# A four-layer graph network on one core: the packed edge table is built and stored before the node rows, from ScalarE's queue

## The chip, the cores and the metric

The kernel is one program on one core of one Trainium2 chip. The metric is the device time of the whole program in microseconds (us); lower is better. TensorE is called PE below, VectorE DVE, ScalarE ACT, GpSimd POOL and SyncE SP. SP, ACT and POOL each can start DMA transfers; the 16 DMA engines of the core carry them.

## The reference, cut to what matters

There are 3125 nodes with 128 features and 53125 directed edges, sorted by destination. Four layers run one after the other; the first one is the one around which the change lies:

```python
h = jnp.maximum(_layernorm(x, axis=-1), 0.0)
msg_in = jnp.concatenate([h[src], h[dst], edge_attr], axis=-1)
msgs = jnp.maximum(msg_in @ mW1 + mb1, 0.0) @ mW2 + mb2
agg = jax.ops.segment_sum(msgs, dst, num_segments=num_nodes)
agg = agg / jnp.clip(cnt, 1.0)[:, None]
...
# layers 2 to 4: segment sums of h[src] over the same edges, unweighted or weighted by edge_weight
```

The later layers use a dense count matrix and a dense weight matrix (nodes by nodes) that the kernel builds from the edge list while it runs the first layer.

## The kernel before

The edges are cut into 104 **quads** of 512 edges (NQ = 104, QE = 512); a quad has four gathers of 128 rows each. The program has two stages around the change.

**Start.** SP loads `x` (25 tiles of 128 nodes, in seven groups j = 0 to 6, the last one of 53 rows) and parts of the edge arrays. ACT's queue loads the two halves of `mW1` and the first 96 rows of `src_l` and `dst_l`. A row of these tiles is one quad: 512 edges and a halo of 112 (624 words, 2496 bytes). Row 103 is shorter. So each of the three arrays (`src`, `dst`, edge weight) comes in as a transfer of 96 rows (QA = NQ // 16 * 16), one of 7 rows and one of 1 row. DVE computes variances (`variance`, `norm`), ACT the roots (`root`), POOL the normed rows (`normed_rows`), PE transposes them (`make_T0`), ACT reads them (`read_T0`), PE multiplies by the first half of `mW1` (`make_P`), ACT reads that (`read_P`) and SP stores it to `p_rows` (`store_P`). Then DVE turns the indices into `idx` (`s_edE`), and POOL may gather from `p_rows`.

**The edge table.** For the dense matrices each edge is packed with its weight in `pw` (4096 * dst + src, and the weight). POOL copies the weight in, DVE the packed index (`s_pk` counts both), and one DMA of 3328 rows of 1024 bytes writes overlapping windows of it to `edge_windows`:

```python
sp.wait_ge(s_pk, 2)
sp.wait_ge(s_pt, 16 * NC)
sp.dma_start(win_tab.rearrange("(q j) c -> q j c", j=32), windows_of(pw_i)).then_inc(s_pst, 16)
```

POOL reads seven groups of it back with seven gathers, in its loop over quads behind the gathers of quad 2 (`if q == 2`), when the store has landed (`s_pst`) and the positions are known (`s_sidx`). DVE decodes them (`unpack`), PE transposes the result (`keys`, 21 transposes), and from quad 4 on each quad also makes one block of the matrices (`blocks`).

**Sweep.** In quad q, PE does `pre(q + 1)` (which waits for the four gathers of quad q + 1 and sums them with the destination part), one half of `blocks(q - 4)`, `seg(q)`, `q_window(q + 4)`, and the other half. ACT does `relu`, DVE adds (`add`, which waits for `q_window`), copies and makes one-hot tiles. Two orders matter: PE runs `keys` at the head of q == 2, behind `pre(2)` and `seg(1)`; DVE runs `unpack` at q == 1, behind `add(0)`, the copy of window 4 and `onehot(2)`. Each engine runs its own instructions in the order in which they are written, with waits on semaphores between them.

Of the kernel before, what the change touches and what calls it, by code (L numbers as in the profile page):

```python
# [5 lines left out]
def gnn_kernel(nc, x_in, src_in, dst_in, ea_in, ew_in, mW1, mb1, mW2, mb2, uW1, ub1, uW2, ub2,  # L6
# [4 lines left out]
    ALU = mybir.AluOpType  # L11
# [3 lines left out]
    N, D = x_in.shape  # L15
# [76 lines left out]
    with ctx:  # L92
# [424 lines left out]
        def _(sp):  # L517
            def tail(tile, array, arrived):
                sp.dma_start(tile[QA:NQ - 1, 0:HALO],
                             bass.AP(array.tensor, QA * QE, [[QE, NQ - 1 - QA], [1, HALO]])).then_inc(arrived, 16)  # L520
                sp.dma_start(tile[NQ - 1:NQ, 0:QR],
                             array[(NQ - 1) * QE:E].rearrange("(a e) -> a e", a=1)).then_inc(arrived, 16)

            def body(tile, array, arrived):
                sp.dma_start(tile[0:QA, 0:HALO], bass.AP(array.tensor, 0, [[QE, QA], [1, HALO]])).then_inc(arrived, 16)

# [11 lines left out]
            sp.wait_ge(s_pad, 6)  # L538
# [40 lines left out]
            sp.wait_ge(s_pad, 7)  # L579
# [158 lines left out]
        def _(pool):  # L738
# [28 lines left out]
            normed_rows(0)  # L767
            pool.memset(zerob[:, :], 0.0).then_inc(s_con, 1)
            normed_rows(1)
            count_up(iota_k[:, :, :], [[1, KCOLS], [0, 2]], base=KBASE).then_inc(s_con, 1)  # L770
            normed_rows(2)
            count_up(iota_l[:, :, :], [[1, 128], [0, 2]]).then_inc(s_con, 1)
            count_up(npio[:, :], [[0, 1]], step=-1).then_inc(s_con, 1)
            normed_rows(3)
            for j in range(4, NC):
                normed_rows(j)

            pool.wait_ge(s_w, 48)
            pool.tensor_copy(pw[:, :, 1], w_l).then_inc(s_pk, 1)
# [8 lines left out]
            for q in range(NQ):  # L788
# [4 lines left out]
                if q == 2:  # L793
# [67 lines left out]
        def _(act):  # L861
# [7 lines left out]
            for k in range(2):  # L869
                act.dma_start(w_m1[:, k, :], mW1[k * D:k * D + D, :]).then_inc(s_wt, 16)  # L870
            for tile, array, arrived in ((src_l, src_in, s_src), (dst_l, dst_in, s_dst)):
                act.dma_start(tile[0:QA, 0:HALO], bass.AP(array.tensor, 0, [[QE, QA], [1, HALO]])).then_inc(arrived, 16)
            act.wait_ge(s_pad, 1)
            for q0, q1 in ((1, QA + 1), (QA + 1, NQ)):
                act.dma_start(prev_i[q0:q1, :], bass.AP(dst_in.tensor, q0 * QE - 2, [[QE, q1 - q0], [1, 2]]))\
                    .then_inc(s_prev, 16)

            act.wait_ge(s_con, 3)
            link(act.activation(sd[:, 0:1], eps[:, 0:1], ACT.Sqrt))

# [35 lines left out]
            pipeline((0, root(0, 0)), (2, read_T0(0)), (3, read_P))  # L916
# [222 lines left out]
        def _(dve):  # L1139
# [7 lines left out]
            dve.memset(prev_i[0:1, :], -1).then_inc(s_pad, 1)  # L1147
            dve.memset(x[:, NT - 1, :], 0.0).then_inc(s_pad, 1)
# [3 lines left out]
            dve.memset(ea_l[QA:NQ, :], 0.0).then_inc(s_pad, 1)  # L1152
# [29 lines left out]

            dve.wait_ge(s_con, 2)
# [12 lines left out]
            dve.wait_ge(s_src, 48)  # L1196
# [819 lines left out]
```

## Time and profile before

| what | value |
|---|---|
| time of the program, median of 3 runs | 1050.0 us (1049.88 to 1053.69) |
| the profiled execution's own time | 1055.58 us |
| its span, first to last instruction | 1053.7 us |
| PE busy (matmul) | 877.1 us, 83% |
| DVE, ACT, POOL busy | 645.6, 503.3, 495.6 us |
| mean granted TensorE clock | 0.963 of full speed |

The span is what the rows below are measured in, from the first instruction. The profiled execution's own time is 1.9 us longer than its span, and 5.6 us longer than the median of the three runs; a sum over rows is made against 1055.58 us and then set beside the median.

### The profile page before, as it was taken

The page shows a single profiled execution, that of the slowest core. Times are in us where ns is not written, and L with a number is a line of the kernel's source. Part 1 is how long each engine was busy: PE and PEld are TensorE (multiplying, and loading weights), DVE is VectorE, ACT ScalarE, POOL GpSimd, SP SyncE. Part 2 cuts the span into 40 slices and gives each one's busy share as a digit, 9 for nine tenths or more (in the row PEclk, how much of TensorE's full clock was granted, in tenths as well). Part 3 has the DMA queues.
Part 4 walks back from the last instruction along what each step waited for, and adds up shares of the span by engine and source line. Part 5 has one row for each costly group of instructions (what it writes and reads, how often), then busy time and mean ns, then how long its engine had stood idle before and what let it go on. Part 6 is the DMA issues. An engine that isn't in the chain of part 4 may idle for free.

```text
span 1053.7 us, 21016 instructions
## 1 busy us (share of the span) xinstructions
PE 877.1 (83%) x7797; PEld 792.2 (75%) x7797; DVE 645.6 (61%) x1759; ACT 503.3 (48%) x1012; POOL 495.6 (47%) x496
## 2 busy tenths in 40 slices
PE   4422887888778787888898888899899999999997
PEld 3422777777777776777887888788788988889786
DVE  5524676867776677667777777787775231213664
ACT  3211455655555555565666666676334300111874
POOL 6457665666666677566666666533411000003111
PEclk9566899999999999999999999999999999999999
DMA  5641355555655558555555555545623787786410
GB/s 145 193 135 45 96 147 147 151 151 149 202 160 147 147 139 138 160 152 157 153 152 148 155 159 153 143 144 169 187 62 141 283 306 285 292 304 206 136 54 23
DMA packets 118795, 169.02 MB, mean 160 GB/s; under 512 B 17248, under 2 KB 85382, under 8 KB 118691
## 3 DMA queue, kind: packets, MB, share of 16 engines
q1 hardware_dynamic: 104405, 138.82, 42.7%
q0 software_dynamic: 13648, 28.21, 10.9%
q8 instruction: 64, 1.05, 0.4%
q10 hardware_dynamic: 638, 0.61, 0.3%
q14 instruction: 40, 0.33, 0.1%
HBM read 109.15 MB, written 58.44 MB: 159 GB/s over the span
## 4 chain that ended last, share of the span: by engine, by line
PE 76%; issue 10%; DMA 4%; DVE 3%; another core or an unknown queue 2%; POOL 2%; ACT 2%; SPq 0%; ACTq 0%; DVEq 0%
PE ps L1883 13%; PE ps L1868 12%; PE ps L1740 12%; PE ps L1706 9%; PE ps L1720 9%; PE ps L1707 8%; PE ps L1738 4%; DMA edge_windows<-room 2%; PE ps L1693 2%; PE ps L1852 2%; POOL h L763 1%; PE ps L1755 1%; DMA x<-in_x 1%; DMA room<-dst_row 1%
## 5 line engine op out<-in xcount | busy, mean ns | idle before, releaser
L784 POOL DMA_INDIRECT room<-p_rows,idx x416 | 413.1, 993 | 235.2 <-issue 99.5
L1740 PE MATMUL ps<-room 128*128 128x100 bf16 x2400 | 193.8, 208 | 59.0 <-issue 57.5
L1740 PEld LDWEIGHTS ps<-room 128*128 128x128 bf16 x2400 | 152.0, 98 | 83.4 <-issue 79.2
L947 ACT ACTIVATE room<-ps 128x400 uint8<-128x400 f32 x200 | 101.1, 506 | 219.1 <-remote 209.6
L1706 PE MATMUL ps<-room,ident 128*128 128x128 f32 x832 | 172.0, 289 | 32.4 <-ACT g L922 15.4
L1738 PE MATMUL ps<-room 128*128 128x100 bf16 x800 | 155.6, 209 | 31.8 <-issue 29.2
L1707 PE MATMUL ps<-room 128*128 128x128 f32 x832 | 164.6, 280 | 0.4 <-issue 0.2
L1286 DVE TENSOR_TENSOR room<-room,Wp 128x800 bf16<-128x800 bf16 x300 | 156.4, 575 | 0.0
L1706 PEld LDWEIGHTS ps<-room,ident 128*128 128x128 f32 x832 | 129.8, 197 | 35.1 <-issue 31.3
L1279 DVE TENSOR_TENSOR room<-iota_k,Kt 128x800 bf16<-128x800 bf16 x100 | 57.4, 574 | 134.6 <-remote 134.4
L1883 PE MATMUL ps<-room,h 128*128 128x256 f32 (+1 forms) x650 | 136.2, 371 | 0.0
L1707 PEld LDWEIGHTS ps<-room 128*128 128x128 f32 x832 | 130.1, 197 | 0.8 <-issue 0.8
L1883 PEld LDWEIGHTS ps<-room,h 128*128 128x128 f32 x650 | 119.2, 190 | 15.2
L1720 PE MATMUL ps<-g 128*128 128x128 f32 x832 | 119.0, 286 | 1.2 <-issue 1.1
L1868 PE MATMUL ps<-wide_room,parts 128*128 128x512 f32 (+1 forms) x520 | 114.5, 374 | 0.6 <-DVE parts L1373 0.6
L953 ACT ACTIVATE room<-ps 128x400 f32<-128x400 f32 x200 | 101.7, 508 | 11.1 <-remote 10.9
L1738 PEld LDWEIGHTS ps<-room 128*128 128x128 bf16 x800 | 78.6, 98 | 37.3 <-issue 34.0
L1868 PEld LDWEIGHTS ps<-wide_room,parts 128*128 128x128 f32 x520 | 91.2, 188 | 18.2 <-DVE parts L1373 1.0
L1720 PEld LDWEIGHTS ps<-g 128*128 128x128 f32 x832 | 102.5, 193 | 2.1 <-issue 1.6
L1268 DVE TENSOR_SCALAR g<-iota,dstT 128x128 f32<-128x128 f32 x416 | 92.7, 309 | 0.0
L928 ACT ACTIVATE room<-room,npio 125x512 bf16<-125x512 bf16 x104 | 76.9, 740 | 19.3 <-issue 10.2
L885 ACT ACTIVATE sd<-mv,eps 128x2 f32<-128x2 f32 (+3 forms) x45 | 13.2, 294 | 141.9 <-DVE mv L1161 141.9
(195 smaller groups left out, 1096.9 us busy)
## 6 DMA issues: line engine op xcount, KB each, us to landing
weight_blocks<-room SPq DMA_DIRECT2D x100, 400.0 KB
room<-weight_blocks SPq DMA_DIRECT2D x12, 3200.0 KB
room<-dst_row SPq DMA_DIRECT2D x104, 128.0 KB
room<-count_blocks SPq DMA_DIRECT2D x8, 1600.0 KB
count_blocks<-room SPq DMA_DIRECT2D x100, 100.0 KB
room<-p_rows,idx POOLq DMA_INDIRECT x416
first_c<-count_blocks SPq DMA_DIRECT2D x4, 1600.0 KB
edge_windows<-room SPq DMA_DIRECT2D x1, 3328.0 KB
```

The costliest lines, as they stand in the source:

```text
L784: return pool.indirect_dma_start(to, None, table, bass.IndirectOffsetOnAxis(ap=at, axis=0))
L947: act.activation(cnt_out[:, u % OUTS, :, at16].rearrange("p h (b w) -> p b h w", w=4), of, ACT.Copy)\
L953: act.activation(w_out[:, u % OUTS, :, at16].rearrange("p h (b w) -> p b h w", w=4), of, ACT.Copy)\
L1268: last = dve.tensor_scalar(oh[:, q % OS, c, :], iota[:, :], dstT[:, q, c:c + 1], None, ALU.is_equal)
L1286: last = dve.tensor_tensor(movw[:, k, a, :, :, :], mov[:, k, :, :, :], blocks_of(Wp[:, a, :], u, KCOLS), ALU.mult)
L1706: pe.matmul(to, ident[:, :], G[:, n % GS, c, :], start=True, stop=False)
L1707: last = pe.matmul(to, sT[:, n % TS, 128 * c:128 * c + 128], Qr[:, n % QS, :], start=False, stop=True)
L1720: last = pe.matmul(bank(2 + n % 2, 128), R[:, n % RS, c, :], oh[:, n % OS, c, :], start=c == 0, stop=c == 3)
L1738: counted = pe.matmul(bank(4 + hh)[:, at], lo, mov[:, k, i, :, t], start=True, stop=True)
L1740: weighed = pe.matmul(bank(6 + hh)[:, at], lo, movw[:, k, a, i, :, t], start=a == 0, stop=a == PARTS - 1)
L1868: last = pe.matmul(to, Hr[:, t, a, :], at[:, k, 0:n], start=a == 0 and t == 0, stop=a == 1 and t == NT - 1)
L1883: last = pe.matmul(bank(dense_bank(j))[:, 256 * half:256 * half + 32 * c], h[:, t, :], ring_w[(2 * j + half) % 3][:, 0:c, t, :], start=t = ...
```

## The change

In words:

- `src_l`, `dst_l` and `w_l` are each loaded by two transfers instead of three: one of 103 rows and one of 1 row. All six are issued from ACT's queue, each behind the memset of its tail rows (those memsets now come first on DVE).
- The loads of `mW1` and of `prev_i` move to SP's queue, behind `x`.
- DVE converts `src` and `dst` and packs them straight behind the variance and scale of group 0, ahead of groups 1 to 6. POOL copies the weights in behind the normed rows of group 0. POOL's constants `npio`, `iota_k`, `iota_l` and `zerob` come behind all normed rows.
- ACT, behind the roots of groups 0 and 1, waits for the packed table and issues its store; only then does it read `T0` of group 0.
- `dst_b` is a copy by ACT instead of a second subtraction by DVE. The memset of `sT` moves to DVE's start.
- POOL's seven gathers from the table come behind quad 0's gathers instead of quad 2's.

```diff
@@ sync
-            tail(src_l, src_in, s_src)
-            tail(dst_l, dst_in, s_dst)
-            body(w_l, ew_in, s_w)
-            tail(w_l, ew_in, s_w)
+            for k in range(2):
+                sp.dma_start(w_m1[:, k, :], mW1[k * D:k * D + D, :]).then_inc(s_wt, 16)
+            for q0, q1 in ((1, QA + 1), (QA + 1, NQ)):
+                sp.dma_start(prev_i[q0:q1, :], bass.AP(dst_in.tensor, q0 * QE - 2, [[QE, q1 - q0], [1, 2]]))\
+                    .then_inc(s_prev, 16)
...
-            sp.wait_ge(s_pk, 2)
             sp.wait_ge(s_pt, 16 * NC)
-            sp.dma_start(win_tab.rearrange("(q j) c -> q j c", j=32), windows_of(pw_i)).then_inc(s_pst, 16)
@@ gpsimd
             normed_rows(0)
+            pool.wait_ge(s_w, 32)
+            pool.tensor_copy(pw[:, :, 1], w_l).then_inc(s_pk, 1)
+            for j in range(1, NC):
+                normed_rows(j)
...
-                if q == 2:
+                if q == 0:
                     pool.wait_ge(s_pst, 16)
                     pool.wait_ge(s_sidx, 1)
@@ scalar
             act.wait_ge(s_con, 3)
             link(act.activation(sd[:, 0:1], eps[:, 0:1], ACT.Sqrt))
+            for n, (tile, array, arrived) in enumerate(((src_l, src_in, s_src), (dst_l, dst_in, s_dst), (w_l, ew_in, s_w))):
+                act.wait_ge(s_pad, n + 1)
+                act.dma_start(tile[0:NQ - 1, 0:HALO], bass.AP(array.tensor, 0, [[QE, NQ - 1], [1, HALO]]))\
+                    .then_inc(arrived, 16)
+                act.dma_start(tile[NQ - 1:NQ, 0:QR],
+                              array[(NQ - 1) * QE:E].rearrange("(a e) -> a e", a=1)).then_inc(arrived, 16)
...
-            pipeline((0, root(0, 0)), (2, read_T0(0)), (3, read_P))
+            root(0, 0)(0)
+            root(0, 0)(1)
+            act.wait_ge(s_pk, 2)
+            act.dma_start(win_tab.rearrange("(q j) c -> q j c", j=32), windows_of(pw_i)).then_inc(s_pst, 16)
+            for j in range(NC):
+                read_T0(0)(j)
+                if j + 2 < NC:
+                    root(0, 0)(j + 2)
+                if j:
+                    read_P(j - 1)
+                if j == NC - 2:
+                    act.wait_ge(s_dr, 1)
+                    act.activation(dst_b, dst_r, ACT.Copy).then_inc(s_dr, 1)
+            read_P(NC - 1)
@@ vector
-            for j in range(NC):
+            dve.wait_ge(*x_of(0))
+            variance(0, 0, x)(0)
+            norm(0, 0)(0)
+            dve.wait_ge(s_src, 32)
+            dve.tensor_copy(src_f, src_l).then_inc(s_srcf, 1)
+            dve.wait_ge(s_dst, 32)
+            link(dve.tensor_copy(dst_f, dst_l))
+            dve.wait_ge(s_srcf, 1)
+            dve.scalar_tensor_tensor(pw_i.rearrange("p (e f) -> p e f", f=2)[:, :, 0], dst_f, 4096.0, src_f,
+                                     ALU.mult, ALU.add).then_inc(s_pk, 1)
+            for j in range(1, NC):
                 dve.wait_ge(*x_of(j))
                 variance(0, 0, x)(j)
-                if j:
+                if j > 1:
                     norm(0, 0)(j - 1)
```

ACT's queue at the start of the program, before. The names are the out and in tiles; `ST` holds `src_l`, `dst_l` and `w_l`, `sd` the roots, `hT` the transposed rows, and the waits are by the semaphores' names:

```order
L870 DMA w_m<-in_L_gnn_mW 128x128 x2
L872 DMA ST<-in_src 96x624
L872 DMA ST<-in_dst 96x624
L875 DMA prev_i<-in_dst 96x2 [waits padding_made]
L875 DMA prev_i<-in_dst 7x2
L879 ACT_TABLE_LOAD
L879 ACTIVATE sd<-eps 128x1 [waits constants_made_then_counts_widened_by_pool]
L885 ACTIVATE sd<-mv,eps 128x4 [waits ln0_variance,act_chain]
L885 ACTIVATE sd<-mv,eps 128x4 [waits ln0_variance] x2
L900 ACTIVATE hT<-ps 128x512 [waits T0_done]
```

The same place in the changed kernel:

```order
L855 ACTIVATE sd<-eps 128x1 [waits constants_made_then_counts_widened_by_pool]
L858 DMA ST<-in_src 103x624 [waits padding_made,act_chain]
L860 DMA ST<-in_src 1x389
L858 DMA ST<-in_dst 103x624 [waits padding_made]
L860 DMA ST<-in_dst 1x389
L858 DMA ST<-in_edge_weight 103x624 [waits padding_made]
L860 DMA ST<-in_edge_weight 1x389
L867 ACTIVATE sd<-mv,eps 128x4 [waits ln0_variance] x2
L901 DMA edge_windows<-room 3328x1x256 [waits edges_packed]
L882 ACTIVATE hT<-ps 128x512 [waits T0_done]
```

The three loads have 103 rows instead of 96, and the table's store stands between the second root and the first read of `T0`.

POOL from the normed rows (`h`) to the first gathers, before:

```order
L763 TENSOR_SCALAR h<-x,rs,nb 128x128 x3
L779 COPY room<-ST 104x624 [waits weights_of_edges_loaded]
L781 COPY room<-room 104x1024 [waits ea_loaded]
L784 DMA room<-p_rows,idx 128x128 [waits p_rows_stored,edges_by_column]
L784 DMA room<-p_rows,idx 128x128 x11
L784 DMA pair<-edge_windows,sidx 128x256 [waits windows_known,edge_windows_stored]
L784 DMA pair<-edge_windows,sidx 128x256 x6
L784 DMA room<-p_rows,idx 128x128 x12
```

and in the changed kernel, in two pieces, the first one behind the normed rows of group 0:

```order
L752 TENSOR_SCALAR h<-x,rs,nb 128x128 x3
L758 COPY room<-ST 104x624 [waits weights_of_edges_loaded]
L752 TENSOR_SCALAR h<-x,rs,nb 128x128 [waits ln0_scale]
...
L769 DMA room<-p_rows,idx 128x128 [waits p_rows_stored,edges_by_column]
L769 DMA room<-p_rows,idx 128x128 x3
L769 DMA pair<-edge_windows,sidx 128x256 [waits windows_known,edge_windows_stored]
L769 DMA pair<-edge_windows,sidx 128x256 x6
L769 DMA room<-p_rows,idx 128x128 x20
```

The copy of the weights now stands ahead of 21 of the 25 normed tiles, and the seven table gathers stand ahead of the gathers of quads 1 and 2.

## Rows read from the trace of the kernel before

**Rows 1.** Chain that ended last, 0 to 130 us: start, us, what

```profile
37.56 23.40 DMA edge_windows<-room
...
61.22 0.94 POOL pair L784
...
68.72 4.39 DMA pair<-edge_windows,sidx
...
73.40 0.64 DVE pair L1293
...
81.80 4.73 PE ps L1747 x21
```

**Rows 2.** Waits, 0 to 150 us: us in total, times, longest

```profile
POOL pair L784 <- DMA edge_windows<-room: 12.3, 1, 12.3
```

**Rows 3.** POOL in order of time: start, us, line, what

```profile
13.23 1.73 POOL L763 TENSOR_SCALAR h<-x,rs,nb 128x128 f32<-128x128 f32 x4
...
25.69 0.76 POOL L779 COPY room<-ST 104x624 f32<-104x624 f32 x1
...
69.97 0.94 POOL L784 DMA_INDIRECT room<-p_rows,idx  x1 [0.30 <-issue]
```

**Rows 4.** ACT in order of time: start, us, line, what

```profile
28.98 0.27 ACT L905 ACTIVATE g<-ps 128x128 f32<-128x128 f32 x1
...
104.92 0.60 ACT L922 ACTIVATE g<-ps 128x512 f32<-128x512 f32 x1 [10.42 <-remote]
```

**Rows 5.** DMA traffic from 1046.5 to 1047.4 us (store of 512 rows)

```profile
q1 hardware_dynamic: 491, 0.25, 91.3%
```

**Rows 6.** DMA traffic from 1050.3 to 1051.6 us (store of 53 rows)

```profile
q1 hardware_dynamic: 54, 0.03, 7.0%
```

**Rows 7.** SP's DMA issues in order of time: start, us of issue

```profile
4.52 1.00 SPq L531 DMA_DIRECT2D x<-in_x  x1
...
38.63 14.45 SPq L594 DMA_DIRECT2D w_m<-in_L_gnn_mW  x1
...
1049.55 0.26 SPq L687 DMA_DIRECT2D out<-h  x1
```

**Rows 8.** DVE in order of time

```profile
13.05 0.87 DVE L1158 BATCH_NORM_STATS2 bn<-x 128x6 f32<-128x128 f32 x4 [0.66 <-DMA x<-in_x]
...
23.91 0.60 DVE L1197 CAST ST<-ST 104x624 f32<-104x624 int32 x1
...
25.33 2.48 DVE L1201 TENSOR_SCALAR room<-ST,sq 104x512 bf16<-104x512 f32 x1
...
40.61 0.17 DVE L1240 CAST sidx<-c 128x7 uint32<-128x7 f32 x1
...
56.27 0.29 DVE L1255 TENSOR_TENSOR ST<-ST,ps 128x128 f32<-128x128 f32 x1 [13.04 <-PE ps L1693]
56.47 0.28 DVE L1262 COPY room<-ps 125x128 f32<-125x128 f32 x1
56.67 0.87 DVE L1268 TENSOR_SCALAR g<-iota,dstT 128x128 f32<-128x128 f32 x4
```

**Rows 9.** Stretches: us, busy of each engine, granted clock, DMA share, GB/s

```profile
4.00:8.00 4.00, 0.00 (x0) 0.00 (x0) 2.06 (x13) 1.55 (x3) 0.00 (x0) 1.00 1.09 229
38.00:53.00 15.00, 5.16 (x22) 4.89 (x23) 5.09 (x18) 3.99 (x6) 8.47 (x9) 0.50 0.81 232
865.00:870.00 5.00, 5.00 (x25) 4.40 (x24) 0.00 (x0) 0.00 (x0) 0.00 (x0) 1.00 1.03 417
```

**Rows 10.** DMA issues by kind: count, KB each, median us to landing

```profile
p_rows<-room SPq DMA_DIRECT2D x6, 256.0 KB, 2.3
```

**Rows 11.** PE in order of time

```profile
51.59 0.79 PE L1706 MATMUL ps<-room,ident 128*128 128x128 f32 x2 [1.92 <-DMA room<-p_rows,idx]
...
89.44 0.39 PE L1707 MATMUL ps<-room 128*128 128x128 f32 x2
```

More of the change, by code:

```diff
@@ L517, in _ @@
         def _(sp):
[L518 to L525, printed above, removed]
             for j in range(NC - 1):
@@ L531, in _ @@
             sp.dma_start(x[0:NR, NT - 1, :], x_in[128 * (NT - 1):N, :]).then_inc(x_of(NC - 1)[0], 16)
[L532 to L535 removed]
+            for k in range(2):
[3 more added lines that the diff above has]
+                    .then_inc(s_prev, 16)
             flat = ea_in.rearrange("e i -> (e i)")
             sp.dma_start(ea_l[0:QA, :], flat[0:QA * 2 * QE].rearrange("(p e) -> p e", e=2 * QE)).then_inc(s_ea, 16)
[L538 removed]
+            sp.wait_ge(s_pad, 7)
             sp.dma_start(ea_l[QA:NQ - 1, :],
@@ L767, in _ @@
             normed_rows(0)
-            pool.memset(zerob[:, :], 0.0).then_inc(s_con, 1)
[L769 to L779, printed above, removed]
+            pool.wait_ge(s_w, 32)
+            pool.tensor_copy(pw[:, :, 1], w_l).then_inc(s_pk, 1)
+            for j in range(1, NC):
+                normed_rows(j)
+            count_up(npio[:, :], [[0, 1]], step=-1).then_inc(s_con, 1)
+            count_up(iota_k[:, :, :], [[1, KCOLS], [0, 2]], base=KBASE).then_inc(s_con, 1)
+            count_up(iota_l[:, :, :], [[1, 128], [0, 2]]).then_inc(s_con, 1)
+            pool.memset(zerob[:, :], 0.0).then_inc(s_con, 1)
             pool.wait_ge(s_ea, 48)
@@ L867, in link @@
                 act.wait_ge(s_act, links[0])
[L869 to L876, printed above, removed]
             act.wait_ge(s_con, 3)
             link(act.activation(sd[:, 0:1], eps[:, 0:1], ACT.Sqrt))
+            for n, (tile, array, arrived) in enumerate(((src_l, src_in, s_src), (dst_l, dst_in, s_dst), (w_l, ew_in, s_w))):
[4 more added lines that the diff above has]
+                              array[(NQ - 1) * QE:E].rearrange("(a e) -> a e", a=1)).then_inc(arrived, 16)
             def root(n, r, parts=TILES):
@@ L1151, in _ @@
             dve.memset(w_l[QA:NQ, :], 0.0).then_inc(s_pad, 1)
-            dve.memset(ea_l[QA:NQ, :], 0.0).then_inc(s_pad, 1)
+            dve.memset(prev_i[0:1, :], -1).then_inc(s_pad, 1)
+            dve.memset(x[:, NT - 1, :], 0.0).then_inc(s_pad, 1)
             def variance(n, r, source=None, parts=TILES):
@@ L1180, in norm @@
                 return stage
+            dve.memset(sT[96:128, :, :], 1.0).then_inc(s_pad, 1)
+            dve.memset(ea_l[QA:NQ, :], 0.0).then_inc(s_pad, 1)
             dve.wait_ge(s_con, 2)
@@ L1187, in _ @@
             link(dve.tensor_scalar(sq[:, :], sq[:, :], -47.0, 0.0, ALU.add, ALU.max))
-            for j in range(NC):
+            dve.wait_ge(*x_of(0))
[9 more added lines that the diff above has]
+            for j in range(1, NC):
                 dve.wait_ge(*x_of(j))
                 variance(0, 0, x)(j)
-                if j:
+                if j > 1:
                     norm(0, 0)(j - 1)
             norm(0, 0)(NC - 1)
-            dve.wait_ge(s_src, 48)
-            dve.tensor_copy(src_f, src_l).then_inc(s_srcf, 1)
-            dve.wait_ge(s_dst, 48)
-            link(dve.tensor_copy(dst_f, dst_l))
             dve.tensor_scalar(dst_r, dst_f[:, 0:QE], sq[0:NQ, 0:1], None, ALU.subtract).then_inc(s_dr, 1)
-            dve.tensor_scalar(dst_b, dst_f[:, 0:QE], sq[0:NQ, 0:1], None, ALU.subtract).then_inc(s_dr, 1)
             dve.wait_ge(s_prev, 32)
@@ L1209, in _ @@
                 .then_inc(s_of, 1)
-            dve.wait_ge(s_srcf, 1)
-            dve.scalar_tensor_tensor(pw_i.rearrange("p (e f) -> p e f", f=2)[:, :, 0], dst_f, 4096.0, src_f,
-                                     ALU.mult, ALU.add).then_inc(s_pk, 1)
-            dve.memset(sT[96:128, :, :], 1.0).then_inc(s_pad, 1)
             for n, (b, to) in enumerate(((2, idx), (1, dstT))):
```

3 lines of the change are left out of this document (removed).

## The prediction

> **What bounds the kernel now.** I first read the chain that ended last. From about 125 us on it is PE, quad after quad, and nothing there is touched by this change. So the change can only move the moment at which the sweep over quads is fully running. Ahead of that the chain stands on one thing: the store of the edge table, 23.4 us from issue to landing, then seven gathers, then 4.4 us from the start of the last gather until it has landed, DVE's decoding from 73.4 us, and PE's 21 transposes from 81.8 us [rows 1]. The waits say the same: POOL stands 12.3 us at its first table gather for the store alone [rows 2]. If PE's `keys` start earlier by some time, the program ends earlier by it, and the other way round.
>
> I then read how the store is released. It waits for the packed table and for all stores of `p_rows`. POOL's weight copy is at 25.7 us, ACT's last read of P ends at 29.25 us, the store is issued at 37.6 us [rows 1, 3, 4]. The new order can issue it as soon as the three edge arrays are there, if they come early. So the question is when the loads land.
>
> **The loads.** Before, each array came as 96 + 7 + 1 rows. Now it is 103 + 1 rows. What a row count does is seen at the program's end, where two stores run alone on SP's queue. The one of 512 rows takes 91.3% of the 16 engines (0.25 MB in 0.9 us) [rows 5]. The one of 53 rows takes 7.0% of them over 1.3 us, which is 1.1 engines, and moves its 27 KB at 27/1.3 = 21 GB/s [rows 6]. A transfer of 53 rows of one kind runs on one engine. The same count is met at the start: the 53-row load of `x`, a tenth of a full one, is issued at 4.52 us, and DVE gets it at 13.05 us [rows 7, 8]. 53 cannot be shared evenly, and neither can 103: both are prime. No row shows 103, so the two bounds are one engine (as 53) and all sixteen (as 512); I take one engine, since 53 is the nearest row in kind.
>
> The Trainium skill, "DMA: Bandwidth & Descriptors", section "Why a DMA increments its semaphore by 16 and not by 1", says that the number of engines is the largest one up to 16 that divides the outermost row count, and names 127 partitions as a case of one engine; by that rule 103 rows also go to one, always the lowest-numbered. The 53-row store agrees (1.1 engines). The same page gives about 27 GiB/s per engine, which would put the last array at 2 + 930/29 = 34 us and the program, by the steps below, near 1060 us; this is an estimate from that page and carries nothing in what follows.
>
> How long one engine takes: three arrays of 103 x 2496 bytes are 771 KB. To these comes what that engine carries of everything else: 98 KB of the six full `x` loads, 27 KB of the 53 rows, and some 34 KB of `mW1` and edge attributes, 930 KB in all, from 2 us on. A busy engine gives at best 417/16 = 26 GB/s, 21 in the 53-row store, and 229/16 = 14 in the start-up when everything loads at once [rows 6, 9]. That makes 38 us at the best rate and 67 us at the worst. At 21 GB/s it is 46 us. The start-up is slower than that and the time behind it, with the other engines idle, may be faster; I take 46 us for the weights, the third array, with `src` near 20 and `dst` near 33 us.
>
> **What waits for it.** DVE stands at `s_src` and `s_dst` behind group 0, with the variances of groups 1 to 6 queued behind. ACT, behind the second root, stands at the table's count of 2, with every read of `T0`, all other roots and all reads of P queued behind, so PE stands too. POOL stands at `s_w`, with 21 normed tiles queued behind. All this ran from 13.2 us before [rows 3].
>
> **The sum.** The weights land at 46, POOL's copy takes 0.8 us [rows 3], so the table is packed at 47 us.
>
> 1. Store of the table: 23.4 us before [rows 1], in company of the gathers (232 GB/s together) [rows 9]. Now the six 256 KB stores of `p_rows` lie beside it. Between 22 (less company) and 32 us (all their bytes one after another); I take 25. Landed at 72 us.
> 2. The other arm: from normed rows of group 1 to the end of the last read of P it was 29.25 - 13.23 = 16 us [rows 3, 4]. POOL's constants leave it, the store's issue and `dst_b` (2.48 us on DVE [rows 8], less on ACT) join. 47 + 16, 4 us for a last `p_rows` store beside the table (2.3 alone [rows 10]) and four gathers at 1.25 us (the steps from 61.22 to 69.97 are 8.75 us for seven [rows 1, 3]) make 72 us, a tie. DVE's way to `sidx` was 40.8 - 23.9 = 16.9 us and loses 6 us of work that is now done earlier or by others [rows 8]; it starts near 59 and ends by 70.
> 3. So the table gathers start at 72 instead of 61.2 us: **+10.8 us**.
> 4. From the first table gather to `keys` it was 81.80 - 61.22 = 20.6 us. The wait of DVE's decoding was the landing alone, since `add(0)` had run at 56.3 us. Now quad 1's gathers stand behind the seven: 11 gathers at 1.25 us, the last starts 12.5 us behind the first, 4.4 us to its landing as before [rows 1], then `pre(1)`, `seg(0)` and `q_window(4)`, 51.59 to 56.27 or 4.7 us [rows 8, 11], `add(0)`, a copy and `onehot(2)`, 56.27 to 57.54 or 1.3 us [rows 8], and the decoding to the transposes, 8.4 us [rows 1]. Together 31.3 us instead of 20.6: **+10.7 us**. The landing may be 2 us quicker with the DMA engines empty, so +8.5 to +10.7.
>
> Costed at nothing: the memsets moved on DVE (DVE waits for `x` and the arrays anyway), the four small issues moved to SP behind `x` (they land long before 46 us; were they late, PE's first transposes would wait for `mW1`), POOL's constants behind the rows (needed when ACT spreads rows, behind 60 us), and SP's 14.45 us of blocked issue behind the table store [rows 7], which disappears but has cover: the layer's weights are needed at quad 40 only.
>
> +21.5 us on 1055.6 is 1077.1 us for a profiled execution; the median of before lies 5.6 lower, so **1071 us**.
>
> **One thing that I leave as it is.** `pre(3)` is over on PE's rows at 89.8 us, but ACT, which waits for it, starts at 104.92 us with "remote" as the reason [rows 4, 11]. 15 us lie there, and no row tells me why. I assume that it comes back after the change. If it does not, it is 15 us less.
>
> **Rivals.**
>
> - *The loads are spread after all (16 engines).* For it: nothing in the code forbids it, and 27 KB is a small witness. Against it: the 7.0%. The arrays would be there near 13 us, when the start-up traffic ends (the last `x` was there at 13.05 [rows 8]). Packed at 14, table landed at 39; the other arm ends at 14 + 16 + 4 + 5 = 39. 39 - 61.2 + 10.7 = -11.5 us: 1038.5 us. This is the one on the other side. It decides when the table gathers can start before 50.5 us, that is, when the weights land before about 25 us. Chance 0.10.
> - *The 15 us do not come back, loads slow.* PE then stands differently ahead of `keys`: the stall came behind a long idle stretch, now `pre(1)` and `pre(2)` run shortly before. 1071 - 15 = 1056 us. Chance 0.12.
> - *The loads partly overlap or the engine is quicker than any row here, so that gain and loss cancel.* It needs 900 KB in 23 us, 39 GB/s, above the 26 seen. 1050 us. Chance 0.03.
>
> **Numbers.** The likeliest, 0.75: 1071 us, its own range 1063 (weights at 38 us) to 1085 (weights at 60 us; the 67 us are for an engine that stays at the start-up rate though the others have gone idle). The range for 8 in 10 reaches down to the second rival: 1054 to 1088. Half a per cent, 5.2 us, is about what a measurement of this kernel can tell from no change. Faster: the first rival and a little, 0.11. Within: the third and the lower edge of the second, 0.05. Slower: 0.84.
>
> **What the new profile would show.** Right: DVE's first cast of `src` near 20 us and its second near 33, each behind a DMA wait; POOL's copy of the weights behind a DMA wait of 30 us or more, at about 46 us; between 20 and 45 us a DMA share near one engine in sixteen (0.06 to 0.1) at some 20 to 26 GB/s; ACT's table store right behind; table gathers from about 72 us; a PE wait for quad 1's gathers, and `keys` about 31 us behind the first table gather. Wrong at the root: the weights there before 25 us with a DMA share near 1. Wrong in size: the step from the weights to the table gathers off 26 us, or `keys` less than 28 us behind them. Wrong by something not seen: a pause other than 15 us behind `keys`.

## The result, and the profile after

The changed kernel took **1093.59 us** (median of 4 runs, 1092.88 to 1095.08) against 1049.94 us (4 runs) for the one before on the same chip: a ratio of **1.0395** (95% interval 1.0374 to 1.0416). Forecast were 1071 us with a range of 1054 to 1088, so the direction was right and the size was not: the loss was 43.6 us, not 21. The profiled execution took 1093.78 us (span 1092.0) against 1055.58: 38.2 us more, where the sum said 21.5.

The chain that ended last in the kernel after (start, us, what), to be held against [rows 1]:

```profile
7.45 12.23 ACTq L860
20.01 23.08 DMA ST<-in_edge_weight
...
66.95 61.41 another core or an unknown queue
137.96 3.23 PE ps L1743 x14
```

The chain no longer runs through the table store but through the load of the weights, and then through 61 us that the profile cannot attribute to anything. `keys` (PE L1743) start at 137.96 instead of 81.80 us. The first part is as forecast. The stretch from 22 to 42 us (busy time of each engine, granted clock, DMA share, GB/s), and POOL and DVE in order of time:

```profile
22.00:42.00 20.00, 1.09 (x4) 0.71 (x4) 5.67 (x31) 0.60 (x2) 2.77 (x4) 1.00 0.07 26
```

```profile
33.92 0.48 DVE L1190 CAST ST<-ST 104x624 f32<-104x624 int32 x1
```

```profile
43.15 0.74 POOL L758 COPY room<-ST 104x624 f32<-104x624 f32 x1 [6.28 <-DMA ST<-in_edge_weight]
...
74.19 1.17 POOL L769 DMA_INDIRECT room<-p_rows,idx  x1 [14.91 <-DMA p_rows<-g]
...
79.42 0.95 POOL L769 DMA_INDIRECT pair<-edge_windows,sidx  x1 [0.30 <-issue]
...
89.43 0.94 POOL L769 DMA_INDIRECT room<-p_rows,idx  x1 [0.30 <-issue]
...
121.92 0.94 POOL L769 DMA_INDIRECT room<-p_rows,idx  x1 [0.30 <-issue]
129.47 1.54 POOL L769 DMA_INDIRECT room<-p_rows,idx  x1 [6.61 <-remote]
```

A DMA share of 0.07 is one engine of 16, the rate is 26 GB/s, and the weights are there at 43.15 us: the three loads of 103 rows go through one engine (before, this copy ran at 25.69 [rows 3]). By the Trainium skill, "DMA: Bandwidth & Descriptors", section "Why a DMA increments its semaphore by 16 and not by 1", 103 outermost rows use one engine, since no number from 2 to 16 divides them; by that, the trace agrees. The estimate from the same page's rate, 34 us, was too early; the row decides. The table gathers start at 79.42 us (61.22 before [rows 1]) and, with 4 gathers ahead of them and 28 behind, POOL gathers back to back from 74.19 to 122.86 us.

What that run does is seen on the other engines. PE, DVE and ACT of the kernel after, in order of time (brackets give the idle time before and what ended it; "remote" and "issue" stand where the profile names no instruction or transfer that did):

```profile
97.56 0.63 PE L1703 MATMUL ps<-room 128*128 128x128 f32 x2
97.99 1.91 PE L1716 MATMUL ps<-g 128*128 128x128 f32 x8
99.69 0.61 PE L1689 MATMUL ps<-w_m,hT 128*128 128x128 f32 x2
```

```profile
128.39 0.29 DVE L1251 TENSOR_TENSOR ST<-ST,ps 128x128 f32<-128x128 f32 x1 [61.44 <-remote]
```

```profile
144.52 0.60 ACT L917 ACTIVATE g<-ps 128x512 f32<-128x512 f32 x1 [0.85 <-PE ps L1703]
```

On PE's rows `pre(1)`, `seg(0)` and `q_window(4)` are over at 100.3 us. DVE's `add(0)`, which waits for just these, starts at 128.39, and DVE's decoding of the table and `keys` are queued behind it: 58.5 us from the first table gather to `keys` instead of 20.6. The other pause, 15 us between PE's rows and ACT's `relu(3)` behind `keys` [rows 4, 11], is gone: `keys` 137.96, `relu(3)` 144.52, or 6.6 us instead of 104.92 - 81.80 = 23.1. The loss at `relu(3)` is 18.2 (start of the table gathers) + 37.9 (from there to `keys`) - 16.5 (from there to `relu(3)`) = 39.6 us, and it changes no more: the sweep has the same period, and POOL's last gather starts at 735.02 instead of 695.67 us, 39.4 later:

```profile
695.67 0.94 POOL L784 DMA_INDIRECT room<-p_rows,idx  x1 [0.30 <-issue]
```

```profile
735.02 0.95 POOL L769 DMA_INDIRECT room<-p_rows,idx  x1 [0.30 <-issue]
```

(first row before, second after). So the profiled executions differ by 16.7 us more than the sum said. The other 5.9 us of the 22.6 us missed in the medians are no part of the mechanism: the execution that was profiled before stood 5.6 us above its median, the one after 0.2, and the forecast was rounded down by 0.5.

### The profile page after: what moved, and what is told of

Same layout as the page of the kernel before. It is cut to its first block, busy times and chain, and to the rows that moved or that the text cites. A ratio compares the mean times of both kernels' runs of the same rounds, so it can differ in the third digit from the quotient of the medians.

```text
span 1092.0 us, 21013 instructions
## 1 busy us (share of the span) xinstructions
PE 882.4 (81%) x7797; PEld 795.5 (73%) x7797; DVE 641.1 (59%) x1758; ACT 503.7 (46%) x1013; POOL 497.0 (46%) x496
## 4 chain that ended last, share of the span: by engine, by line
PE 76%; issue 9%; another core or an unknown queue 6%; DVE 4%; DMA 2%; ACTq 1%; ACT 1%; POOL 0%; DVEq 0%
PE ps L1879 12%; PE ps L1736 12%; PE ps L1864 12%; PE ps L1716 9%; PE ps L1702 9%; PE ps L1703 9%; PE ps L1734 4%; DMA ST<-in_edge_weight 2%; PE ps L1689 2%; PE ps L1848 2%; ACTq L860 1%; PE ps L1638 1%; PE ps L1751 1%; PE ps L1750 1%
## 5 line engine op out<-in xcount | busy, mean ns | idle before, releaser
L1734 PE MATMUL ps<-room 128*128 128x100 bf16 x800 | 156.4, 209 | 21.5 <-issue 21.0
L1716 PE MATMUL ps<-g 128*128 128x128 f32 x832 | 122.2, 291 | 1.0 <-issue 0.9
L948 ACT ACTIVATE room<-ps 128x400 f32<-128x400 f32 x200 | 101.8, 509 | 13.0 <-remote 12.3
L1716 PEld LDWEIGHTS ps<-g 128*128 128x128 f32 x832 | 105.7, 199 | 2.0 <-issue 1.7
```

Of the source, the lines that this page charges most:

```text
L948: act.activation(w_out[:, u % OUTS, :, at16].rearrange("p h (b w) -> p b h w", w=4), of, ACT.Copy)\
L1716: last = pe.matmul(bank(2 + n % 2, 128), R[:, n % RS, c, :], oh[:, n % OS, c, :], start=c == 0, stop=c == 3)
L1734: counted = pe.matmul(bank(4 + hh)[:, at], lo, mov[:, k, i, :, t], start=True, stop=True)
```

## The experiments

The theory from the two traces: **PE's completions reach the other engines late while POOL issues gathers back to back, and come when the run of gathers stops.** (A completion is the count on a semaphore by which PE tells the others that a group of matmuls is done.) Rivals: PE's low clock after idle time, PE's instruction fetch, or no such thing and only a chain of landings. The traces speak against instruction fetch: no packet of an instruction queue moves between 85 and 140 us in the kernel after, nor between 56 and 108 us in run 1, and yet PE goes on inside both stretches (at 108.05 and 90.49 us), so no late instruction ended these pauses. All experiments ran on other chips, on which the kernel before took 1054 to 1062 us; each ratio is to the kernel before in the same comparison.

**1. Loads split again.** The changed kernel; each array in 96 + 7 + 1 rows, still from ACT's queue:

```diff
-act.dma_start(tile[0:NQ - 1, 0:HALO], bass.AP(array.tensor, 0, [[QE, NQ - 1], [1, HALO]])).then_inc(arrived, 16)
+act.dma_start(tile[0:QA, 0:HALO], bass.AP(array.tensor, 0, [[QE, QA], [1, HALO]])).then_inc(arrived, 16)
+act.dma_start(tile[QA:NQ - 1, 0:HALO], bass.AP(array.tensor, QA * QE, [[QE, NQ - 1 - QA], [1, HALO]])).then_inc(arrived, 16)
```

> The changed kernel with each edge array loaded in 96 + 7 + 1 rows again, on the same queue and in the same place. One-engine theory: the weights land by 15 us instead of 43, the table is stored near 16 us, and the table's gathers start near 40 us. If nothing else cost anything, the program would take 1038 us (11 us below the one before). By the theory that PE's completions reach the others only when POOL's run of 39 gathers back to back ends, keys still stand some 58 us behind the first table gather, and the program takes 1050 to 1056 us. By the theory that the time was lost on something else than the loads (the new order of ACT, say), it stays above 1075 us.

Measured: 1.0133 (1.0106 to 1.016), above the 1050 to 1056 us that the theory was given (some 1064 us on that base) and below the 1075 us of its rival. So the 103-row form alone is worth 1.0395 - 1.0133 = 2.6%, some 27 us. But the first table gather starts at 49.13 us, 12 us earlier than before, and the kernel is still 1.3% slower than before. `keys` start at 108.65, 59.5 us behind that gather. ACT, PE, POOL and DVE of this run, in order of time:

```profile
57.42 0.60 ACT L919 ACTIVATE g<-ps 128x512 f32<-128x512 f32 x1 [6.01 <-remote]
89.07 0.60 ACT L919 ACTIVATE g<-ps 128x512 f32<-128x512 f32 x1 [31.05 <-remote]
```

```profile
67.64 1.06 PE L1718 MATMUL ps<-g 128*128 128x128 f32 x8
90.49 0.77 PE L1704 MATMUL ps<-room,ident 128*128 128x128 f32 x2 [21.57 <-issue]
```

```profile
86.60 0.94 POOL L769 DMA_INDIRECT room<-p_rows,idx  x1 [0.30 <-issue]
89.31 0.94 POOL L769 DMA_INDIRECT room<-p_rows,idx  x1 [1.77 <-remote]
```

```profile
99.04 0.29 DVE L1253 TENSOR_TENSOR ST<-ST,ps 128x128 f32<-128x128 f32 x1 [59.76 <-PE ps L1691]
```

PE's rows of `pre(1)` end near 67.8 us. `relu(1)` starts at 89.07, 1.5 us behind the end of the last gather of the run (86.60 + 0.94), and POOL, which waits for the same count, goes on at 89.31. From 69 to 90 us only POOL works. The count itself comes late; ACT was idle. So 1038 us, the forecast's value for loads that are spread, does not come even when they are. Not every completion in the run is late: `relu(0)` starts at 57.42 us, 2.2 us behind the end of PE's rows of `pre(0)` (55.25) and with POOL gathering all the while.

**2. Table gathers behind quad 2 in the changed kernel** (`if q == 2` for `if q == 0`, nothing else).

> The changed kernel with the seven table gathers behind quad 2 again. By the theory of a chain of landings, the table gathers start at 74 + 15 = 89 us, keys follow 20.6 us later, near 110 instead of 138 us, and the program takes 1066 us. By the theory of the gather run, its length (seven and eight quads, 39 gathers from 74 us on) is the same, keys stay near 137 us, and the time stays at 1090 to 1095 us.

Measured: 1.0402 (1.037 to 1.0435), the same as the whole change. The place of the seven gathers is worth nothing here. The chain of landings expected 27 us; `keys` stand at 139.00 us, because the run is as long as ever. The row:

```profile
129.33 0.29 DVE L1251 TENSOR_TENSOR ST<-ST,ps 128x128 f32<-128x128 f32 x1 [62.19 <-remote]
```

**3 and 4. A short lead at the start**, in both kernels:

```diff
-if q >= GS:
-    pool.wait_ge(s_pre, q - GS + 1)
+ahead = 3 if q < 12 else GS
+if q >= ahead:
+    pool.wait_ge(s_pre, q - ahead + 1)
```

> The kernel before; its only edit is that POOL may be three quads ahead of pre instead of eight while q is under 12, so that it stops between gathers early on. By the theory of the gather run, the pause of 15 us behind keys (relu(3) at 104.92 us, though pre(3) was over at 89.8) goes, relu(4) comes 8 to 15 us earlier, and the program takes 1035 to 1042 us. By the rival (PE's clock or its instruction fetch after the idle stretch) POOL's lead does not matter: 1048 to 1052 us. If the shorter lead starves PE, it is above 1055 us.

> The changed kernel with POOL's lead at three quads while q is under 12. By the theory of the gather run, the first run is 4 + 7 + 8 = 19 gathers from 74 to 99 us instead of 39, DVE's add(0) starts near 101 instead of 128 us, keys near 110 instead of 138, and the program takes 1064 to 1070 us. By the rival (clock, instruction fetch, anything on PE itself) add(0) stays near 128 us and the time at 1090 to 1095 us.

(The ring holds six quads, not eight as the first of these texts says; what they work out is not touched by it.) Measured: before 1.0032 (1.0013 to 1.005), after 1.0367 (1.034 to 1.0393). Both expected times were missed (1035 to 1042 and 1064 to 1070 us). The two places moved the way that was expected, in the changed kernel by less: `add(0)` at 108.80 us (expected near 101, 128.39 without the edit) and `keys` at 118.48 (expected near 110). ACT's `relu` in the kernel before with the short lead, and then in the changed one:

```profile
89.25 0.60 ACT L923 ACTIVATE g<-ps 128x512 f32<-128x512 f32 x1
...
131.09 0.60 ACT L923 ACTIVATE g<-ps 128x512 f32<-128x512 f32 x1 [2.86 <-remote]
150.47 0.60 ACT L923 ACTIVATE g<-ps 128x512 f32<-128x512 f32 x1
```

```profile
167.22 0.60 ACT L918 ACTIVATE g<-ps 128x512 f32<-128x512 f32 x1 [2.52 <-remote]
187.33 0.60 ACT L918 ACTIVATE g<-ps 128x512 f32<-128x512 f32 x1
```

`relu(3)` comes at 89.25 instead of 104.92 us: the 15 us pause is gone. When POOL comes to quad 12, the lead opens to six, POOL gathers the difference in one run, and a step of 19.4 us (20.1 in the changed kernel) stands there instead of 6.2. The pause belongs to the filling of the ring, wherever it is filled.

**5. The run cut by stops.** The changed kernel; POOL waits for the landing of each of the quads 0 to 5:

```diff
     rows_at(G[:, q % GS, c, :], P_tab, idx[:, q, c:c + 1]).then_inc(s_gat[q % GS], 16)
+if q < 6:
+    pool.wait_ge(s_gat[q], 64)
```

> The changed kernel; its only edit is that POOL, behind the four gathers of each of the quads 0 to 5, waits until they have landed (some 2 us each), so that its run of 39 gathers is cut into pieces. (POOL's ring holds six quads; the expectation of the run with the short lead said eight by mistake.) By the theory that PE's completions come late while POOL issues gathers back to back, s_pre(1) comes in or near such a stop, below 100 instead of at 106.6 us, keys near 115 to 122 instead of 138, and the time falls by 5 to 15 us to a ratio of 1.025 to 1.035. If the length of the run does not matter (the cause lies in PE, its clock, or in the DMA traffic), keys stay near 138 us, and the stops cost up to 12 us: 1.04 to 1.05.

Measured: 1.0372 (1.0333 to 1.0412), just above the expected 1.025 to 1.035; `add(0)` at 101.74 instead of 128.39 us, and `keys`:

```profile
111.47 3.95 PE L1745 MATMUL ps<-ident,pair 128*128 128x128 f32 x21 [3.11 <-DVE pair L1302]
```

26.5 us earlier. ACT's `relu` follow PE's rows again, until POOL fills the ring without stops:

```profile
100.42 0.60 ACT L919 ACTIVATE g<-ps 128x512 f32<-128x512 f32 x1 [14.57 <-PE ps L1705]
...
128.52 0.60 ACT L919 ACTIVATE g<-ps 128x512 f32<-128x512 f32 x1 [5.30 <-PE ps L1705]
159.55 0.60 ACT L919 ACTIVATE g<-ps 128x512 f32<-128x512 f32 x1 [14.40 <-remote]
```

So the length of the run sets when PE's completions come; the total hardly moves, because the gain is given back at 128 to 160 us. (`relu(1)` came at 100.42, just outside "below 100".)

**6. Filler on PE.** The changed kernel; 16 more matmuls ahead of each of `q_window(4)` to `q_window(7)`, so that PE does not stand idle behind `pre(1)`:

```diff
+for _ in range(16 if LEAD <= n < LEAD + 4 else 0):
+    pe.matmul(q_bank(n), hT[:, at:at + 128], w_m1[:, 1, :], start=True, stop=True)
```

> The changed kernel with 16 further matmuls of 128x128x128 (the same as the one that follows, into the same bank) ahead of each of q_window(4) to q_window(7), so that PE has work of some 4 to 7 us behind pre(1) and pre(2). By the rival that PE's completions are late because PE stands idle and cold behind them, s_pre(1) comes at once behind its row, near 98 instead of 106.6 us, keys 10 us or more earlier, and the ratio falls to 1.02 to 1.03. By the theory of the gather run nothing comes earlier: 1.039 to 1.050.

Measured: 1.0402 (1.0367 to 1.0438). PE in order of time (each of the 16 matmuls is two records), and ACT's `relu(1)`:

```profile
99.34 2.85 PE L1690 MATMUL ps<-w_m,hT 128*128 128x128 f32 x20
102.72 0.27 PE L1690 MATMUL ps<-w_m,hT 128*128 128x128 f32 x1 [0.54 <-issue]
104.13 0.27 PE L1690 MATMUL ps<-w_m,hT 128*128 128x128 f32 x1 [1.14 <-issue]
...
134.21 3.83 PE L1690 MATMUL ps<-w_m,hT 128*128 128x128 f32 x32
```

```profile
108.34 0.60 ACT L917 ACTIVATE g<-ps 128x512 f32<-128x512 f32 x1 [22.62 <-remote]
```

PE's rows of `pre(1)` end at 97.8 us and PE works on without a gap to 102.2, and still `relu(1)` comes only at 108.34 (106.63 without the filler): idleness behind `pre(1)` is not the cause. The filler shows more than it was made for. It waits for nothing, and yet, after 20 records at full pace, PE starts one record in some 2.6 us (ten from 102.72 to 126.3 us) for as long as POOL gathers and some 4 us longer (POOL's run ends at 122.3). The next filler, outside a run, takes 3.83 us for all 32 records. So in a run of gathers it is not only the news of PE's work that is late; PE itself nearly stands. A single record takes 0.27 to 0.37 us there, so the granted clock (0.60 on the mean from 102.2 to 126.6 us) does not explain gaps of up to 3.3 us. (`add(0)`, at 129.34 us here, decides nothing in this run: its `q_window(4)` stands behind the filler and has its row at 128.71.)

**7. Runs of eight gathers in the sweep.** The kernel before:

```diff
-if q >= GS:
-    pool.wait_ge(s_pre, q - GS + 1)
+if q >= GS and q % 2 == 0:
+    pool.wait_ge(s_pre, min(q - GS + 2, NQ))
```

> The kernel before; its only edit is that POOL waits for pre once for two quads (for the later of the two slots) and then issues eight gathers in one run. In the sweep POOL issues four gathers (5.0 us), stops for 1.17 us, and the period is 6.17 us a quad. If PE's completions come only in the stops and one stop can pass two of them, the period falls towards (10 + 1.2) / 2 = 5.6 us and the program takes 0.95 to 0.97 of before. If PE needs a stop for each quad, because its steps wait for ACT and DVE in turn, the stop gets twice as long and the ratio is 0.99 to 1.03. If PE's own work set the period, it stays: 0.995 to 1.01.

Measured: **1.2252** (1.2207 to 1.2296), far outside every case that was expected. POOL's waits from 150 to 360 us (us in total, times, longest), first in the kernel before, then here:

```profile
POOL room L784 <- remote: 46.4, 34, 1.5
```

```profile
POOL room L784 <- PE ps L1707: 78.2, 12, 7.5
```

34 stops of 1.36 us, one a quad, have become 12 of 6.5 us, one for two quads. One of these stops:

```profile
191.84 0.94 POOL L784 DMA_INDIRECT room<-p_rows,idx  x1 [6.97 <-PE ps L1707]
```

```profile
191.61 0.60 ACT L922 ACTIVATE g<-ps 128x512 f32<-128x512 f32 x1 [1.89 <-PE ps L1707]
203.44 0.60 ACT L922 ACTIVATE g<-ps 128x512 f32<-128x512 f32 x1 [3.51 <-remote]
```

The run from 191.84 us ends near 202, and the next `relu` comes at 203.44, 1.4 us behind it; the second `pre` of the pair is done only in the stop. In the run itself PE's matmuls stand apart by up to 1.25 us, as in experiment 6. A part of the loss may be the clock: from 150 to 360 us the mean granted clock is 0.81 here and 1.00 in the kernel before, and how much of the longer stops that makes was not taken apart. That the stop of 1.36 us in the kernel before is the same delay in small is argued from this run and the next, not shown by itself.

**8. Other work on POOL.** The kernel before; five index patterns of some 0.35 us each on a spare tile behind each quad's gathers:

```diff
+if q >= GS:
+    for _ in range(5):
+        link(count_up(spare[:, :], [[1, 200]]))
```

> The kernel before; its only edit is that POOL, behind the four gathers of each quad from 6 on, writes a spare tile five times (index patterns, some 2 us in all) before it waits for pre. If only gathers hold PE's completions back, pre arrives while POOL writes and the period is 5.0 + 2 = 7.1 us: 1.08 to 1.10. If any work on POOL holds them back, it is 5.0 + 2 + 1.2 = 8.3 us: 1.18 to 1.22.

Measured: 1.0834 (1.0801 to 1.0867, from two executions), the first case. POOL in order of time:

```profile
246.31 1.79 POOL L748 IOTA spare<- 128x200 f32 x5
248.49 0.96 POOL L785 DMA_INDIRECT room<-p_rows,idx  x1 [0.39 <-POOL spare L748]
...
253.54 1.78 POOL L748 IOTA spare<- 128x200 f32 x5
```

POOL goes straight from its writes to the next gather: the count for which it waits has come while it wrote. Other work on POOL does not hold PE's completions back; gathers do.

**9. The early store alone, and the stop that it takes away.** Run 1 with the table gathers behind quad 2; and the same with `pool.wait_ge(s_pre, 3)` ahead of the table gathers.

> The changed kernel with each edge array in 96 + 7 + 1 rows and the table gathers behind quad 2: what is left is the store issued early by ACT. The store was no longer what the table gathers wait for in the run with the split loads alone (it was there before the first gather of quad 0 at 43.9 us). So the gathers run 12 + 7 from 44 us on, the first of the table near 59 us, against 61.2 us before. By the chain of landings keys come 2 us earlier than before and the program is at 0.996 to 1.000 of before. If the early order costs something else on ACT or DVE, it is above 1.005.

> The run with the split loads and the table gathers behind quad 2, with one stop: POOL waits for pre(2) ahead of the table gathers (before, it stood there anyway, for the store, from 48 to 61 us). By the theory that this stop was worth something in the kernel before, since PE's three first pre, seg(0) and DVE's add(0) came through in it, the table gathers start near 67 instead of 59.7 us, the stops of 7.8, 12.7 and 5.6 us between 92 and 132 us shrink to those of before (4.1), and the ratio falls from 1.012 to 1.002 to 1.008. If the stop does nothing for PE, it costs its 7 us: 1.018.

Measured: 1.0119 (1.0083 to 1.0155), a miss for the chain of landings, and with the stop 1.0072 (1.0048 to 1.0097), as expected. The two ratios were taken on different chips, and their difference, 0.0047, is barely clear of the noise. In the first, POOL never stops between 44.6 and 93 us, and then it stands at a full ring. POOL's waits from 30 to 150 us without and with the stop:

```profile
POOL room L769 <- PE ps L1705: 17.7, 3, 11.7
...
POOL room L769 <- remote: 8.3, 2, 6.8
```

```profile
POOL room L769 <- remote: 9.9, 6, 2.5
POOL pair L769 <- PE ps L1706: 7.7, 1, 7.7
```

26.0 us of waiting against 17.6. The 12.3 us for which POOL stood at the table store in the kernel before [rows 2] were not lost: in them PE finished `pre(0)` to `pre(2)`, and DVE `add(0)` at 56.27 [rows 8]. A table that comes earlier takes this stop away. The places show it far more plainly than the total does: with the one stop, of 7.7 us, `add(0)` starts at 60.86 instead of 99.59 us and `keys` at 85.62 instead of 109.21. The total moves by only some 5 us, so most of these 24 us are given back later.

**10. The same without the stop, the store behind ACT's last read of P.**

> The run with the split loads and the table gathers behind quad 2 (1.012), with the table store issued by ACT behind its last read of P instead of ahead of the first. If the store's packets are what delayed the p_rows stores, the first gather of quad 0 starts near 34 to 36 us again instead of 44, the table is there near 60, POOL stands before it as in the kernel before, and the ratio is 0.997 to 1.003. If the new order on POOL, DVE and ACT was the cause, the first gather stays near 44, the table near 62, and the ratio stays at 1.008 to 1.015.

Measured: 1.0026 (1.0 to 1.0052). The first gather starts at 39.19 us, between the two cases: 5.4 of the 10.6 us of delay (44.56 with the early store, 34.00 in the kernel before) go with the place of the store. What the rest is was not tried; the store still lies beside the last, small store of `p_rows`, which lands in 7.6 us here and in 3.3 us in the kernel before. The issues of `p_rows` (count, KB each, median us from issue to landing) with the early store; with the late one the last number is 2.3:

```profile
p_rows<-room SPq DMA_DIRECT2D x6, 256.0 KB, 10.8
```

The Trainium skill, "DMA: Bandwidth & Descriptors", section "Rules for kernel authors", advises to issue a DMA early and wait for it late. Here the early 3.3 MB store made six transfers that were needed sooner land in 10.8 instead of 2.3 us [rows 10]; the rows decide. And although the table gathers now start at 55.32 instead of 61.22 us, nothing is gained: `add(0)` waits until 93.79 us.

**11. A shorter lead in the whole sweep** (the kernel before; the condition and the wait with 3, 4 or 2 in place of GS).

> The kernel before; its only edit is that POOL stays at most three quads ahead of pre in the whole sweep, instead of six (the ring itself is left at six). In the sweep POOL's four gathers and one stop make the period of 6.17 us; the last six quads, for which nothing is gathered any more, take 5.3 us each. By the theory that POOL's gathers and the stops behind them are the clock, a shorter lead shortens the long run at the start by 3 x 5 us and turns three of the last quads from 5.3 into 6.17 us: 8 to 12 us less, a ratio of 0.988 to 0.993. If the lead is needed to cover the gathers' landing, the period grows and the ratio is above 1.01. The run with three quads for q under 12 alone stood at 1.003, with the pause moved to where the lead grew to six.

> The kernel before with a lead of four quads in the whole sweep. By the theory each quad of lead costs some 3 us as long as landing is covered: 0.994 (0.992 to 0.997), between 0.991 at three and 1 at six. If three is the only lead that helps, it is 0.998 or more.

> The same with a lead of two quads. By the theory another 3 to 4 us less, 0.984 to 0.990, if gathers (5.0 us) and their landing (2.2 us) still fit into two periods of 6.17 us; above 1.01 if they do not.

Measured: lead 3 **0.9908** (0.9882 to 0.9934), lead 4 **0.992** (0.989 to 0.995), both as expected; lead 2 0.9973 (0.9955 to 0.9991), a miss. The kernel before, a stretch of the sweep and one of the quads for which nothing is gathered any more:

```profile
184.60:190.80 6.20, 5.17 (x60) 4.71 (x60) 6.13 (x14) 3.88 (x9) 4.04 (x4) 1.00 0.50 149
698.00:718.00 20.00, 20.00 (x241) 19.07 (x241) 19.36 (x62) 17.12 (x39) 0.00 (x0) 1.00 0.45 141
```

PE is idle 1 us in each 6.2 while POOL gathers and never when it does not, with DMA traffic of the same size. With two quads of lead POOL's stops grow already at 30 to 150 us; the longest wait for PE there is 8.4 us, against 3.0 with four. Why two is too few (landing, or the waits at `keys`) was not taken apart.

**12. The changed order with these edits.** Run 9 with the stop and a lead of 3; run 10 with the stop and a lead of 4.

> The changed order with split loads, table gathers behind quad 2, the stop for pre(2), and a lead of three quads in the whole sweep. By the theory the two edits add: 1.0072 less 0.009 = 0.996 to 1.000, that is, not better than the kernel before with a lead of three (0.991), since the first gather still starts 10 us later. If the early store were worth something once the pause is gone, it would be under 0.990.

> The run with the late store by ACT (1.003), and with it POOL's stop for pre(2) ahead of the table gathers and a lead of four quads. By the theory the pause ahead of keys goes, and what stands against the kernel before with a lead of four (0.992) is the first gather, at 39 instead of 34 us, and so the table gathers, near 62 instead of 60 us: 0.990 to 0.996. If the early table is worth its 6 us, 0.984 to 0.989.

Measured: 0.9939 (0.9921 to 0.9958), a little below the expected 0.996, and 0.9993 (0.9977 to 1.0009), above the expected 0.990 to 0.996. The pause ahead of `keys` is gone in both (`keys` at 83.89 and 83.30 us); where the second one loses the rest of its time was not found. Neither is better than the kernel before with a lead of 3 or 4, which is the fastest version found.

## Why the prediction was wrong

- **One engine for 103 rows: right**, and the size too: weights at 43.15 us (46 forecast), 26 GB/s. `src` and `dst` were not seen at 20 and 33 us, since DVE got to both casts only from 33.92 us on: they stand behind the scale of group 0, which waits for ACT's root, and ACT stood still while it issued its loads (below).
- **Step 1, the table store: right.** It was issued at 43.92 us, and no engine waited for it.
- **Step 2, the other arm: failed by 7 us.** The last `p_rows` store was allowed 4 us. It took 16.0: ACT's last read of P ended at 58.15 us (63 forecast, since the weights were earlier), and POOL's first gather stood until 74.19, where 67 was forecast. Beside the table store the median landing of the `p_rows` stores was 10.6 us, and five of SP's issues took 12.28 us. This term of the sum was mis-sized, by 12 us; 5 us that were forecast too long ahead of it hid a part.
- **Step 3: +10.8 forecast, +18.2 measured**, by step 2 alone.
- **Step 4, from the first table gather to `keys`: failed.** 31.3 us forecast, 58.5 measured. The rows were taken as if PE's steps were done for the others when their row ends. `pre(1)`, `seg(0)` and `q_window(4)` took the forecast time on PE's rows (94.4 to 100.3 us); DVE learned of them 28 us later. Experiments 5, 7, 8 and 9 changed the run of gathers itself and moved the delay with it; experiments 1, 2 and 6 left the run and changed the loads, the place of the table gathers and PE's idleness, and the delay stayed. The run of gathers does it, not the loads, not landings, not PE's idleness; by what means is open.
- **The pause left as it was: the wrong half of the choice.** It was assumed to come back behind `keys`; it was gone from there (6.6 instead of 23.1 us from `keys` to `relu(3)`, -16.5) and came ahead of `keys`, larger. The forecast said that no row told why it lay there. It lay where POOL fills its ring in one run; the change moved that run ahead of `keys`. Held together: 7.4 (step 2) + 27.2 (step 4) - 16.5 (this) = 18.1 us, against 39.6 - 21.5 = 18.1 missing at `relu(3)` (16.7 at the program's end).
- **The base: 5.9 us of the miss.** The sum was taken from a profiled execution of 1055.58 us to the median by 5.6 us and rounded down; the profiled one after lay at its median.
- **The rivals.** "The loads are spread" was put at 1038.5 us; experiment 1 made exactly that true and gave 1.0133, some 1064 us on the same base. It would have failed by the same steps: its first gather starts at 43.91 us, where this rival's sum has 34 (step 2), and `keys` come 59.5 us behind the first table gather, where it has 31.3 (step 4), the stop of 12.3 us being gone with the early table. "The 15 us do not come back" was right in its letter and wrong in its sum.
- **Costed at nothing.** The moved memsets, SP's small issues and POOL's constants show in no wait ahead of 74 us; right as far as seen, not tried one by one. But ACT's issues were left out of the sum altogether, and they held ACT for 31 us; that was hidden behind the load of the weights.

A shorter reading of the whole: **from the first gather on, POOL is the clock.** Its first gather starts 40.2 us later (74.19 for 34.00). Its 13th starts at 61.22 us before and at 89.43 after, 28.2 later, since the stop at the table store is not made; its last one 39.4 later. The 11.2 us between are longer stops at a full ring, for PE to catch up. The experiments fit this account in the places that moved. They do not fit it in all sizes: the times of experiments 1, 3, 4 and 5 and of the second run of 12 came out longer than expected from it, and it does not say why a lead of two is worse than three.

## What to carry to other kernels

When an engine's wait ends long after the row that releases it, look at what POOL does in between: here, during a long unbroken run of indirect gathers, PE's completions came late and PE's own work nearly stood, and a wait that seemed idle was what let PE catch up. Try a smaller lead of the prefetch than the ring allows: three or four quads instead of six made this kernel 0.8 to 0.9% faster. And a transfer that is issued early competes with what is needed sooner; count what lands beside it.

## What the runs showed of the hardware

- **PE's completions and gathers.** With four gathers in a run (5.0 us) POOL stands some 1.4 us for `pre` each time; with eight (10 us), 6.5 us. In a run of 39, completions came up to 28 us behind PE's rows. They come some 1 to 2 us behind the last gather of a run, sometimes later (6.4 us in the kernel after), and some get through inside a run: at 106.63 us in the kernel after, 9 us late, and nearly at once for `relu(0)` in run 1 (57.42) and the first transposes in the kernel before (started at 81.80, read by ACT at 83.57). What sets these apart is not known.
- **PE's own pace.** Matmuls that wait for nothing ran 20 records without a gap and then one in some 2.6 us while POOL gathered; outside a run 32 took 3.83 us (experiment 6). Whether the issuing on POOL or the gathers' packets hold PE back is open: the two end within some 2 to 4 us of each other.
- **Issuing can block.** With one DMA engine taking the 103-row loads, a transfer of a single row kept ACT for 12.23 (the chain above) and 13.23 us, ahead of its second square root:

```profile
7.45 12.23 ACTq L860 DMA_DIRECT2D ST<-in_dst  x1
20.01 13.23 ACTq L860 DMA_DIRECT2D ST<-in_edge_weight  x1
33.29 0.30 ACT L867 ACTIVATE sd<-mv,eps 128x4 f32<-128x4 f32 x1 [31.06 <-issue]
```

It cost nothing here, since the weights came later still; with other work on that queue it would have.
